# ScalarE subtracts half of the score maxima, GpSimd takes inverse roots, scores come in halves

## The reference

```python
x = x + tanh(g_xattn[0]) * convolution_attention(ctx, ctx, layernorm(x), ssm_kernel, D)
x = x + tanh(g_ffn[0])   * base_and_lora(layernorm(x))        # top-8 of 64 ranks
x = x + tanh(g_xattn[1]) * cross_attention(layernorm(x), ctx)
x = x + tanh(g_ffn[1])   * experts(layernorm(x))              # shared one and top-2 of 8
```

```python
q = qdq(x) @ qdq(wq).T + bq
k, v = split(cond @ wkv.T + bkv)
attn = softmax(q @ k.T / sqrt(16))      # over 128 keys of the same block
out = qdq(attn @ v) @ qdq(wp).T + bp
```

## Time and profile before

| | |
|---|---|
| median of the runs | 219.73 us |
| profiled execution | 218.84 us, of which 216.7 are its span |
| busy: TensorE, VectorE, ScalarE, GpSimd | 176.3, 164.2, 108.5, 81.5 us |
| mean granted clock of TensorE | 0.965 of 2.4 GHz |
| chain that ended last, by engine | TensorE 50%, VectorE 18%, ScalarE 12% |

### The profile page before, as it was taken

The page is one execution under the profiler, slowest core; times in us unless marked ns, Lnnn a source line. Parts: engine busy times, 40 slices in busy tenths (PEclk is TensorE's granted clock), DMA queues, the critical chain, the costliest instruction groups (busy, mean ns, idle before and its releaser), DMA issues.

```text
span 216.7 us, 3606 instructions
## 1 busy us (share of the span) xinstructions
PE 176.3 (81%) x1156; PEld 111.4 (51%) x1156; DVE 164.2 (76%) x465; ACT 108.5 (50%) x288; POOL 81.5 (38%) x114
## 2 busy tenths in 40 slices
PE   0369999989989989885788788798787959979962
PEld 0236555558555556542455556565566327636531
DVE  0698999994178999979689999999936853575634
ACT  2440343211423245641588789887975473543621
POOL 1386557024755550593121204420220373065100
PEclk9999999999999999999599999999999788999998
DMA  6989970000000000000000000000000057665772
GB/s 182 395 208 374 363 258 15 3 0 0 0 0 2 3 0 2 0 0 2 3 0 0 5 0 5 3 0 0 3 0 3 2 97 145 76 120 113 161 164 97
DMA packets 22625, 15.17 MB, mean 70 GB/s; under 512 B 17648, under 2 KB 21328, under 8 KB 22096
## 3 DMA queue, kind: packets, MB, share of 16 engines
q1 hardware_dynamic: 21968, 13.94, 24.1%
q10 hardware_dynamic: 640, 1.02, 1.3%
HBM read 9.68 MB, written 1.07 MB: 50 GB/s over the span
## 4 chain that ended last, share of the span: by engine, by line
PE 50%; DVE 18%; ACT 12%; DMA 7%; issue 7%; SPq 4%; DVEq 0%
PE PS L1648 7%; PE PS L1316 5%; PE PS L1318 5%; PE PS L1317 5%; DMA X<-x 4%; PE PS L1404 4%; PE PS L1666 3%; PE PS L1380 3%; DMA R<-R 3%; SPq L426 3%; PE PS L1338 3%; ACT R L651 3%; ACT R L646 2%; PE PS L1480 2%; PE PS L1347 2%
## 5 line engine op out<-in xcount | busy, mean ns | idle before, releaser
L496 POOL TENSOR_SCALAR R<-QT,SM 128x256 bf16<-128x256 f32 x32 | 15.8, 508 | 28.0 <-DVE SM L1100 19.6
L1269 DVE TENSOR_TENSOR R<-R,PS 128x512 bf16<-128x512 f32 (+1 forms) x17 | 11.7, 687 | 15.4 <-ACT R L773 8.1
L1022 DVE TENSOR_REDUCE SM<-PS 128x8 f32<-128x1024 f32 x16 | 18.8, 1213 | 3.0 <-PE PS L1480 1.9
L1648 PE MATMUL PS<-R 128*128 128x512 bf16 x64 | 17.1, 388 | 3.6 <-DMA R<-R 3.6
L1494 PE MATMUL PS<-CON,R 128*128 128x128 f32 x128 | 19.0, 281 | 1.2 <-ACT R L651 1.2
L472 POOL TENSOR_TENSOR R<-R,CON 128x256 f32<-128x256 f32 x16 | 9.6, 620 | 24.7 <-PE PS L1480 15.5
L651 ACT ACTIVATE R<-PS 128x512 f32<-128x512 f32 x32 | 18.4, 600 | 0.9 <-PE PS L1494 0.8
L337 POOL TENSOR_TENSOR R<-CT 128x512 f32<-128x512 f32 x12 | 13.8, 1154 | 12.2 <-PE PS L1318 6.7
L773 ACT ACTIVATE R<-PS 128x512 f32<-128x512 f32 x17 | 10.1, 596 | 14.8 <-PE PS L1648 14.8
L549 ACT ACTIVATE LNV<-MV,EPSC 128x1 f32<-128x1 f32 (+1 forms) x26 | 7.6, 293 | 17.6 <-DVE MV L945 11.2
L1494 PEld LDWEIGHTS PS<-CON,R 128*128 128x128 f32 x128 | 14.5, 143 | 3.5 <-issue 3.0
(11 more groups left out here) (152 smaller groups left out, 428.1 us busy)
## 6 DMA issues: line engine op xcount, KB each, us to landing
WST<-w SPq DMA_DIRECT2D x3, 1024.0 KB, 11.3
T_R<-lagged SPq DMA_DIRECT2D x2, 768.0 KB, 7.7
X<-x SPq DMA_DIRECT2D x2, 512.0 KB, 6.9
CT<-ctxr SPq DMA_DIRECT2D x1, 1024.0 KB, 7.5
y<-X SPq DMA_DIRECT2D x8, 128.0 KB, 1.9
WKV<-wkv SPq DMA_DIRECT2D x1, 512.0 KB, 9.9
WQP<-wqp ACTq DMA_DIRECT2D x1, 512.0 KB, 6.2
R<-sw SPq DMA_DIRECT2D x3, 128.0 KB, 4.4
```

Source lines behind the costliest of these rows:

```text
L496: nc.gpsimd.tensor_scalar(XB[:, u % XS, j, :], MX[:, b, :], GG[:, b, e:e + 1], 1.0, ALU.mult, ALU.mult).then_inc(e_xb, 1)
L1022: V_.tensor_reduce(MX1[:, b % 2, 8 * c:8 * c + 8], S4[:, 8 * c:8 * c + 8, :], AX.X, ALU.max, negate=True).then_inc(a_mx, 1)
L1648: ins = M(PS[:, 2 + 2 * (v % 2) + n, :], lhs, rhs, start=(k == 0), stop=(k == NL - 1))
```

## The change

- ScalarE subtracts for heads 8 to 15 (banks 2 and 3), in eight instructions a block; VectorE for heads 0 to 7, in one.
- The scores of every block come in two halves, with a count for each half. The first half waits for VectorE's subtraction of the block before, the second for ScalarE's, and on TensorE the second stands behind the first two groups of values. Transposes `k` = 2 and 3 wait for ScalarE.
- The inverse roots of the attention from block 3 on, and of the fourth stage for blocks 0 to 4, are computed by GpSimd: it adds the small constant to the variance and takes the power -0.5. They stand in its loop ahead of the keys, and behind it between the last rows. ScalarE keeps the others.
- GpSimd writes a constant of -0.5 at the start, and the counts that wait for its first writes grow by one.
- VectorE's mean and variance for the attention are taken for block `s+4` at the end of step `s`, instead of for block `s+3` behind the subtraction.

```diff
@@ -106,6 +106,7 @@
         EPSC = sb("EPSC", [P, 1])
+        HALFM = sb("HALFM", [P, 1])
         WS = sb("WS", [P, 4])
@@ -434,6 +435,7 @@
         def _(pool):
             nc.gpsimd.memset(ONES[:, :], 1.0).then_inc(ones_s, 1)
+            nc.gpsimd.memset(HALFM[:, :], -0.5).then_inc(ones_s, 1)
             nc.gpsimd.memset(EPSC[:, :], EPS).then_inc(ones_s, 1)
@@ -464,10 +466,8 @@
                     pool.wait_ge(kev, 2 * NG)
-                if b == 2:
-                    pool.wait_ge(a_s0, 2)
-                elif b > 2:
-                    pool.wait_ge(a_s, b - 2)
+                if b >= 2:
+                    pool.wait_ge(a_s, 2 * (b - 1))
                 for c in range(2):
@@ -482,6 +482,20 @@
+            def root(b, done, n):
+                nc.gpsimd.tensor_scalar(LNV[:, b:b + 1], MV[:, b, 1:2], EPS, None, ALU.add).then_inc(done, 1)
+                pool.wait_ge(done, n + 1)
+                nc.gpsimd.tensor_tensor(RS[:, b:b + 1], LNV[:, b:b + 1], HALFM[:, 0:1], ALU.pow).then_inc(done, 1)
+            def a_root(b):
+                pool.wait_ge(a_ln, 2 * (b + 1))
+                root(b, a_rp, 2 * (b - 3))
+            def m_root(b):
+                pool.wait_ge(m_ln, 2 * (b + 1))
+                root(b, m_rp, 2 * b)
             def expert_rows(u):
@@ -521,13 +535,21 @@
             for b in range(2, NB):
+                if b + 1 < NB:
+                    a_root(b + 1)
+                if b == NB - 1:
+                    m_root(0)
                 block_keys(b)
...
                     finish(b - 5)
-            for b in range(NB - 5, NB - LATE):
-                finish(b)
+            m_root(1)
+            finish(NB - 5)
+            m_root(2)
+            finish(NB - 4)
+            m_root(3)
+            m_root(4)
             expert_rows(0)
@@ -636,14 +658,14 @@
-            def a_last_subtract(b):
+            def a_late_subtract(b):
...
                     act.wait_ge(a_et, 4 * (b - 1))
-                for j in range(4):
-                    h = 12 + j
-                    nc.scalar.activation(SS[:, b % 2, h, :], PS[:, 3, P * j:P * j + P], ACT.Identity,
+                for j in range(8):
+                    h = 8 + j
+                    nc.scalar.activation(SS[:, b % 2, h, :], PS[:, 2 + j // 4, P * (j % 4):P * (j % 4) + P], ACT.Identity,
                                          bias=MX1[:, b % 2, h:h + 1]).then_inc(a_sa, 1)
...
             def a_exp(b, k):
@@ -678,7 +700,7 @@
             def m_rstd(b):
-                rstd(m_ln, 2 * (b + 1), b, b + 1, m_rs, 2 * b)
+                rstd(m_ln, 2 * (b + 1), b, b + 1, m_rs, 2 * (b - 5))
             def m_zt_(b):
@@ -721,25 +743,20 @@
-            a_rstd(3)
             for s in range(NB):
...
                     a_exp(s - 1, 0)
-                if s >= 5:
-                    m_rstd(s - 5)
                 if s >= 3:
...
                     a_exp(s - 1, 1)
-                a_last_subtract(s)
+                a_late_subtract(s)
                 if s + 2 < NB:
                     a_q_(s + 2)
-                if 1 <= s < NB - 3:
-                    a_rstd(s + 3)
                 if s >= 1:
@@ -776,7 +793,6 @@
             a_exp(NB - 1, 1)
-            m_rstd(NB - 5)
             a_exp(NB - 1, 2)
@@ -784,7 +800,6 @@
             o_q_(NB - 2)
-            m_rstd(NB - 4)
             o_ev_(NB - 2)
@@ -998,7 +1013,10 @@
                 if k == 0:
-                    dve.wait_ge(a_rs, 2 * (b + 1))
+                    if b < 3:
+                        dve.wait_ge(a_rs, 2 * (b + 1))
+                    else:
+                        dve.wait_ge(a_rp, 2 * (b - 2))
                     s.mark(V_.tensor_scalar(AZ[:, a, :], X[:, b, :], MV[:, b, 0:1], RS[:, b:b + 1],
@@ -1015,21 +1033,17 @@
             def a_max(b, c):
-                if b == 0:
-                    dve.wait_ge(a_s0, c + 1)
-                else:
-                    dve.wait_ge(a_s, b)
+                dve.wait_ge(a_s, 2 * b + c + 1)
                 V_.tensor_reduce(MX1[:, b % 2, 8 * c:8 * c + 8], S4[:, 8 * c:8 * c + 8, :], AX.X, ALU.max, negate=True
...
-            def a_subtract(b, c):
-                a, ks = b % 2, slice(8 * c, (8, 12)[c])
-                dve.wait_ge(a_mx, 2 * b + c + 1)
+            def a_subtract(b):
+                a = b % 2
+                dve.wait_ge(a_mx, 2 * b + 1)
                 if b >= 2:
-                    dve.wait_ge(a_et, 4 * (b - 2) + 2 * c + 2)
-                n = (8, 4)[c]
-                V_.tensor_tensor(SS[:, a, ks, :], S4[:, ks, :], MX1[:, a, ks].unsqueeze(2).to_broadcast([P, n, P]),
+                    dve.wait_ge(a_et, 4 * (b - 2) + 2)
+                V_.tensor_tensor(SS[:, a, 0:8, :], S4[:, 0:8, :], MX1[:, a, 0:8].unsqueeze(2).to_broadcast([P, 8, P]),
                                  ALU.add).then_inc(a_sub, 1)
...
             def o_norm(b, k):
@@ -1069,7 +1083,10 @@
             def m_rows(b):
-                dve.wait_ge(m_rs, 2 * (b + 1))
+                if b < 5:
+                    dve.wait_ge(m_rp, 2 * (b + 1))
+                else:
+                    dve.wait_ge(m_rs, 2 * (b - 4))
                 V_.tensor_scalar(MX[:, b, :], X[:, b, :], MV[:, b, 0:1], RS[:, b:b + 1], ALU.subtract, ALU.mult
@@ -1104,7 +1121,7 @@
                     a_max(0, 1)
-                    a_subtract(0, 0)
+                    a_subtract(0)
                 if route:
@@ -1151,14 +1168,9 @@
                     a_max(s, 1)
-                    a_subtract(s, 0)
-                a_subtract(s, 1)
-                if new and s >= 1:
-                    a_stats(s + 3, 0)
+                    a_subtract(s)
                 if norm:
                     o_norm(s - 2, 0)
-                if new and s >= 1:
-                    a_stats(s + 3, 1)
                 if norm:
@@ -1179,10 +1191,14 @@
                     m_stats(s - 4, 0)
+                if s + 4 < NB:
+                    a_stats(s + 4, 0)
                 if new:
...
                     m_stats(s - 4, 1)
+                if s + 4 < NB:
+                    a_stats(s + 4, 1)
                 if new:
@@ -1454,38 +1470,26 @@
-            def first_scores(half):
-                pe.wait_ge(a_q, 2)
-                pe.wait_ge(kbd, 2)
-                pe.wait_ge(x1, NB)
-                if half == 1:
-                    pe.wait_ge(f_me, NB - 1)
+            def a_scores(b, half):
+                pe.wait_ge(a_q, 2 * (b + 1))
+                pe.wait_ge(kbd, 2 * (b + 1))
+                if b == 0:
+                    pe.wait_ge((x1, f_me)[half], (NB, NB - 1)[half])
+                else:
+                    pe.wait_ge((a_sub, a_sa)[half], (b, 8 * b)[half])
                 for c in range(2):
                     for r in (2 * half, 2 * half + 1):
-                        rows = slice(VW * r, VW * r + VW)
-                        ins = M(PS[:, r, 2 * P * c:2 * P * c + 2 * P], AQH[rows, 0, c, :],
-                                KBD[rows, 0, c].rearrange("p s m -> p (s m)"), start=True, stop=True)
-                ins.then_inc(a_s0, 1)
-            def a_scores(b):
-                pe.wait_ge(a_q, 2 * (b + 1))
-                pe.wait_ge(kbd, 2 * (b + 1))
-                pe.wait_ge(a_sub, 2 * b)
-                pe.wait_ge(a_sa, 4 * b)
-                for c in range(2):
-                    for r in range(4):
                         rows = slice(VW * r, VW * r + VW)
...
             def a_turn(b, k):
-                if k < 3:
-                    pe.wait_ge(a_sub, 2 * b + k // 2 + 1)
+                if k < 2:
+                    pe.wait_ge(a_sub, b + 1)
                 else:
-                    pe.wait_ge(a_sa, 4 * (b + 1))
+                    pe.wait_ge(a_sa, 8 * b + 4 * (k - 1))
                 if b == 0:
@@ -1526,7 +1530,7 @@
                 elif b < NB - 1:
-                    pe.wait_ge(a_sub, 2 * NB - 1)
+                    pe.wait_ge(a_sub, NB)
                 else:
@@ -1571,7 +1575,7 @@
                 if NB <= s <= NB + 1:
-                    first_scores(s - NB)
+                    a_scores(0, s - NB)
                 if 2 <= s <= NB + 1:
@@ -1614,12 +1618,14 @@
                 if s + 1 < NB:
-                    a_scores(s + 1)
+                    a_scores(s + 1, 0)
                 if s >= 3:
...
                     a_values(s - 1, 2)
+                if s + 1 < NB:
+                    a_scores(s + 1, 1)
                 if s >= 3:
@@ -1637,8 +1643,7 @@
                 elif n == 0 and v == 0:
-                    pe.wait_ge(a_sub, 2 * NB)
-                    pe.wait_ge(a_sa, 4 * NB)
+                    pe.wait_ge(a_sa, 8 * NB)
                 elif n == 0:
```

More of the change, by code:

```diff
@@ L271, in build @@
             "a_q"))
-        a_s0 = sem("a_s0")
         a_sa = sem("a_sa")
@@ L310, in build @@
             "e_acc"))
+        a_rp, m_rp = sem("a_rp"), sem("m_rp")
         e_xa, e_xd = sem("e_xa"), sem("e_xd")
@@ L543, in _ @@
             act.dma_start(lagged, KP[:, :]).then_inc(L["lag"], 16)
-            act.wait_ge(ones_s, 2)
+            act.wait_ge(ones_s, 3)
```

(2 more changed lines are left out.)

## The result

The changed kernel takes 226.58 us (median of 4 runs, 225.76 to 228.66) against 219.91: the ratio is 1.033, 95% interval 1.028 to 1.039. It is 6.7 us slower, where 1.5 was forecast. The profiled execution took 225.76 us for a span of 223.6, and 218.84 for 216.7 before: 6.9 more.

The account below looks back on a forecast made before the run. VectorE was taken as full, ScalarE and TensorE right behind. Periods +1.0, block 7's subtraction +0.96 and the root leaving ScalarE -0.45 gave +1.5 on 219.73: 221.2 us, own range 220.0 to 222.6, wide range 217.0 to 223.6.

Parts of the forecast that it names:

- half 0 to 2.05, output transpose 0.2, two value groups 0.57, half 1 from 2.83 to 3.90: TensorE's order in block 3, in us from the start of ScalarE's subtraction, with no wait before the output transpose.
- periods 4 and 5: Times between ScalarE's subtraction starts, blocks 3 to 4 and 4 to 5: forecast 7.77 us each, from 7.65 and 7.97.
- rival D: Slower by TensorE's clock: low level lasts longer or falls again on the stage, +2 on the forecast, 223.2 us; chance 0.12.
- period 1: ScalarE's subtraction start in block 0 to that in block 1: both halves at low clock, +1.0, so 7.45 us.
- period 3: ScalarE's subtraction start in block 2 to that in block 3: 7.12 us, 1.6 us of waiting for VectorE not fully replaced.
- a half costs a whole: TensorE's scores: two row strips take as long as four, so halves add about 1.07 us in each of blocks 1 to 7.
- ScalarE's wait for VectorE replaced by waits for TensorE: In block 3 ScalarE's wait for VectorE's quantising gives way to three small TensorE waits, 0.6 us together; net +0.12.
- the tail: After block 7's subtraction starts: +0.96 us for the longer subtraction, about 0.45 back from the root leaving ScalarE.
- rival C: Slower by GpSimd: a slow power makes a root 4.7 us, about 225 us; decides from 0.65 us a root; chance 0.08.
- Rival A: Faster: ScalarE packs without the small TensorE waits, each period falls to its own work, 3.0 faster, 216.7 us; chance 0.22.
- Rival B: About even: ScalarE's waits for TensorE are half as long, 0.3 a block less over five periods, 219.7 us; chance 0.13.
- where it is full: VectorE's statistics moved to the end of the step before cost nothing in busy steps; step 0's extra set is free.

Follow-up runs that it names:

- q_first_late_b: The changed kernel with ScalarE's scaling of the queries ahead of its eight subtractions in steps 3 to 5 alone: 223.5 us, ratio 1.010 to the kernel before.
- o_behind: The changed kernel with TensorE's output transpose moved from ahead of the first values to behind the second half of the scores: 222.9 us, ratio 1.015.
- q_first: The changed kernel with ScalarE's scaling of the queries ahead of its eight subtractions in all steps: 226.9 us, ratio 1.034 to the kernel before.
- fill_after: The changed kernel with 18 extra identity transposes on TensorE ahead of the second scores: 225.8 us, ratio 1.035 to the kernel before.
- whole: The changed kernel with the scores of blocks 1 to 7 in one set again, behind both subtractions: 224.1 us, ratio 1.021 to the kernel before.

## Why the prediction was wrong

**The step that failed**: "half 0 to 2.05, output transpose 0.2, two value groups 0.57, half 1 from 2.83 to 3.90". The output transpose waits for the scaling of the queries of the next but one block (`pe.wait_ge(a_q, 2 * (b + 6))`, since both use one bank), which the change puts 1.0 us later. Before, the scores themselves waited for ScalarE's subtraction, so this wait was hidden behind them; with half 0 free to start early it came to the front, and value groups, half 1, projection and last values queued behind it. I had named what the new waits of the diff hold up, and not what the old ones do once the work ahead of them moves. The periods that hold this wait, 4 to 6, are 0.71, 0.73 and 0.89 us over the forecast at full clock, 2.3 of the 5.8 us by which the stage missed. `q_first_late_b` and `o_behind` take the wait away, and periods 4 and 5 fall to 7.94 to 7.99, 0.2 over the forecast; over the whole stage they bring 1.6 and 1.0 us, since each of them makes another period longer.

**The low clock** (rival D, given 0.12) is the second: 0.66 us in period 1 and 2.47 in period 5 of the profiled run. I had put the first block at the low level up to 109 us, with the turn behind the halves at 2.4 GHz again; it lasted to 112, over the turns. Whether the new wait brings the low clock of period 5 isn't settled: the profiles of `q_first`, `o_behind` and `q_first_late_b`, without the wait, have none there, but `fill_after`, with it, has none either.

**The rest**, 0.34 us, lies in periods 2, 3 and 7. Right were: period 3 (7.18 for 7.12); a half costs a whole (1.13 and 1.15); ScalarE's wait for VectorE replaced by waits for TensorE; the tail (0.57 for 0.51). A root took 0.9 us for my 0.6. That is past the 0.65 from which rival C was to count, but it cost next to nothing: root 3 ended at 167.72 and VectorE's rows of block 3 began at 167.75, at most 0.1 later than without a wait. Rival A, the faster kernel, needed ScalarE packed, with 7.2 us in periods 4 and 5. It wasn't: its output rows waited 4.4 us for the projection, and even `whole`, free of halves, took 7.8. Rival B, with smaller waits than forecast, is out with it.

**The parts.** The forecast charged the eight subtractions 1.0 us a block and set the vanishing waits for VectorE against it; they cost 8.4 us on top of the roots by medians. In the profiled runs it is 7.6: the periods 5.2, and from block 7's subtraction to the router 2.2, of which 1.0 stand before TensorE falls to its low level at about 163 us. The roots were taken as 0.43 us a block on ScalarE and the moved statistics as nothing "where it is full": alone they bring 4.1 us, 2.7 of them with the statistics. The halves were taken as 1.07 a block: they cost 2.5 us on top of the roots, with or without the subtractions, and nothing alone.

## What to carry to other kernels

When an edit lets an instruction start earlier, read every wait of the instructions queued behind it, old ones too: what stood hidden behind the removed wait is late next. Work moved from an engine that is 98% busy to one at 87% gains nothing if it costs more there (here 0.25 us a head against 0.15); moving small work out of their way (one-element roots to GpSimd, which is busy for 38% of the span, and statistics into an idle step) gained 4 us. Parts that look additive needn't be: the halves were free while VectorE was the bound and cost 2.5 us once it wasn't.

## What the hardware showed beside that

A power of one element in each of 128 partitions took GpSimd 0.57 us, an add of the same shape 0.22 to 0.25. By the Trainium skill, page "GPSIMD Engine Reference", section "3.1 Elementwise — side-by-side cycle accounting", dispatching an instruction takes VectorE about 156 ns, and GpSimd goes through two software hops where VectorE has one; the page gives GpSimd's dispatch no figure and has no price for a power, so these two durations neither confirm nor contradict it. Eight matmuls with a contraction of 32 rows took 1.13 us on two row strips, sixteen on four strips 1.15. Runs of the same kernel differ by how long TensorE has its low level: the change took 225.8, 227.4 and 228.7 us at mean clocks of 0.947, 0.939 and 0.931. With the rest at full clock that is 23.7, 27.5 and 31.3 us at the low level; by this estimate each microsecond there costs about 0.4 us. Eighteen extra transposes raised the mean clock of the profiled run from 0.957 to 0.975 with the roots alone and hardly changed the median (215.7 and 215.4).
